# A gated recurrent stage rebuilt on pairs of tiles, in a one-core transformer kernel

## The reference

```python
def step(S, inp):                      # one chunk of 64 rows, for every batch and head
    qb, kb, vb, bb = inp               # bb: running sum of log-sigmoid gates in the chunk
    qg = qb * exp(bb) * scale
    kd = kb * exp(-bb)
    A = where(mask, einsum('bhtd,bhsd->bhts', qg, kd), 0)
    o = einsum('bhts,bhsv->bhtv', A, vb) + einsum('bhtd,bhdv->bhtv', qg, S)
    b_last = bb[:, :, -1:, :]
    kg = kb * exp(b_last - bb)
    S = S * exp(b_last) + einsum('bhtd,bhtv->bhdv', kg, vb)
    return S, o
...
o = o * rsqrt(mean(o * o) + EPS) * rms_w      # per head of 64 columns
o = (o * silu(x @ Wg)) @ Wo
x = x + layernorm(o);  stream = layernorm(x)  # input of the attention layers
```

## Time and profile before

| | |
|---|---|
| median of 3 runs | 548.07 us (546.76 to 548.08) |
| profiled execution | 544.76 us, its span 542.8 us |
| PE busy | 481.8 us (89%), 4512 matmul instructions |
| DVE busy | 407.8 us (75%), 957 |
| ACT busy | 354.8 us (65%), 953 |
| POOL busy | 217.1 us (40%), 188 |
| chain that ended last | PE 50%, DVE 20%, ACT 13%, issue 10%, others 7% |

### The profile page before, as it was taken

The page is one execution under the profiler, slowest core; times in us unless marked ns, Lnnn a source line. Parts: engine busy times, 40 slices in busy tenths (PEclk is TensorE's granted clock), DMA queues, the critical chain, the costliest instruction groups (busy, mean ns, idle before and its releaser), DMA issues.

```text
span 542.8 us, 13374 instructions
## 1 busy us (share of the span) xinstructions
PE 481.8 (89%) x4512; PEld 318.4 (59%) x4512; DVE 407.8 (75%) x957; ACT 354.8 (65%) x953; POOL 217.1 (40%) x188
## 2 busy tenths in 40 slices
PE   3988999997489999999997699799999999987893
PEld 1555655665246767676766356576767676763463
DVE  4799999998377989898985244778888888862456
ACT  3677898886246777777776143476878787752424
POOL 6032111112266666666666001456565656540002
PEclk9999999999589999999999989989999999999798
DMA  6900000000000000000000000000000000000002
GB/s 144 319 0 2 2 2 2 2 2 2 0 1 7 6 12 6 12 6 12 8 11 7 11 0 2 1 1 12 6 11 7 12 7 11 6 13 10 1 0 79
DMA packets 19338, 10.26 MB, mean 19 GB/s; under 512 B 11532, under 2 KB 18504, under 8 KB 19272
## 3 DMA queue, kind: packets, MB, share of 16 engines
q1 hardware_dynamic: 18952, 9.40, 6.2%
q0 software_dynamic: 320, 0.01, 0.2%
HBM read 6.25 MB, written 1.05 MB: 13 GB/s over the span
## 4 chain that ended last, share of the span: by engine, by line
PE 50%; DVE 20%; ACT 13%; issue 10%; DMA 2%; POOL 2%; SPq 2%; DVEq 0%; ACTq 0%; POOLq 0%
PE p_turn L476 11%; PE p_sc L476 9%; PE p_qk L476 8%; PE p_vo L476 8%; DVE ss L1428 4%; DVE neg_max L1445 4%; ACT sq L1036 4%; PE p_mix L476 4%; PE p_turn L704 3%; PE p_sc L744 2%; ACT qk_t L1055 2%; DVE hid L1230 2%; DVE probs L1452 2%; ACT probs_t L1068 2%; POOL qr L426 2%
## 5 line engine op out<-in xcount | busy, mean ns | idle before, releaser
L417 POOL TENSOR_TENSOR qr<-rot 128x1024 f32<-128x1024 f32 x32 | 76.5, 2389 | 104.8 <-DVE rot L1420 104.8
L426 POOL TENSOR_TENSOR qr<-qr,inv 128x1024 f32<-128x1024 f32 x32 | 60.9, 1902 | 41.2 <-issue 38.5
L476 PE MATMUL p_qk<-wqkv_sb,h_t 128*128 128x512 f32 x128 | 63.6, 622 | 5.6 <-ACT sq L1036 4.9
L1428 DVE TENSOR_REDUCE ss<-sq 128x16 f32<-128x1024 f32 x32 | 39.0, 1219 | 34.3 <-ACT sq L1036 34.3
L384 POOL TENSOR_TENSOR og<-og,silu 128x256 f32<-128x256 f32 x16 | 11.6, 726 | 98.9 <-DVE og L1285 98.9
L1061 ACT ACTIVATE probs<-probs 128x512 f32<-128x512 f32 x64 | 40.4, 631 | 13.8 <-DVE probs L1452 13.0
L1075 ACT ACTIVATE o_t<-p_vo 128x512 f32<-128x512 f32 x32 | 19.1, 598 | 42.7 <-PE p_vo L769 42.7
L1452 DVE TENSOR_TENSOR probs<-p_sc,neg_max 128x512 f32<-128x512 f32 x64 | 44.3, 692 | 2.2
L1445 DVE TENSOR_REDUCE neg_max<-p_sc 128x4 f32<-128x512 f32 x64 | 43.7, 683 | 1.8 <-PE p_sc L476 1.8
L704 PEld LDWEIGHTS p_turn<-consts,qr 128*128 128x128 f32 x256 | 29.5, 141 | 24.1 <-POOL qr L426 13.9
L1420 DVE TENSOR_TENSOR rot<-p_qk,cos_t 128x1024 f32<-128x1024 f32 x32 | 38.6, 1207 | 3.4 <-PE p_qk L476 3.4
(11 more groups left out here) (166 smaller groups left out, 1174.8 us busy)
## 6 DMA issues: line engine op xcount, KB each, us to landing
wqkv_sb<-in_L_ffn_wqkv SPq DMA_DIRECT2D x1, 1536.0 KB, 9.7
hcat<-middle SPq DMA_DIRECT2D x32, 32.0 KB
out_x<-pong SPq DMA_DIRECT2D x8, 128.0 KB, 1.9
hcat<-middle SPq DMA_DIRECT2D x32, 31.8 KB
x_in<-in_L_attn_x SPq DMA_DIRECT2D x2, 448.0 KB, 5.2
w_sb<-in_L_ffn_w SPq DMA_DIRECT2D x1, 682.0 KB
cos_base<-rotary_cos SPq DMA_DIRECT2D x1, 512.0 KB, 5.5
sin_base<-rotary_sin SPq DMA_DIRECT2D x1, 512.0 KB, 6.3
```

Source lines behind the costliest of these rows:

```text
L417: pool.tensor_tensor(o, a, b[:, :, ::-1, :], ALU.add).then_inc(s["add_ready"], 1)
L426: pool.tensor_tensor(a, a, inv[:, :].unsqueeze(2).to_broadcast([P, 2 * AH, DH]), ALU.mult).then_inc(s["qr_ready"], 1)
L476: return pe.matmul(o, w, m, start=start, stop=stop, skip_group_check=skip)
L1428: dve.tensor_reduce(ss[:, :], sq[:, :].rearrange("p (h e) -> p h e", e=DH), AX.X, ALU.add).then_inc(s["ss_ready"], 1)
```

## The change

Only the recurrent stage and its seam to attention are changed.

- The unit is now a pair of tiles, one of each batch (256 rows), so there are 8 steps in place of 16, and element-wise instructions are twice as wide.
- Scores, key-value, intra and state products are made for each batch, head and chunk apart: 16 products each per pair, with 32 or 64 contraction rows, on their own part of the array. The padding and the four 32-row instructions of `decay_q` are gone. Within `intra_scores` and `state_outputs` the second half of the heads waits for the first (`at_done`, `half_done`).
- The two low-rank gate matrices are multiplied once at the start (`combine_gate_weights`), and rms_w is folded into Wo.
- The state is kept so that the key product with `kd` serves it (u = S + kd^T v, then S = u * decay, the second on POOL); `kg` and its decay are gone. silu is an exp, ln, exp chain (x clamped at -87 by `gate_input` on DVE).
- `normalise_x`, `normalise_f`, `decay_log`, the state decays and the product of gate and value move from DVE to POOL. The two rotary tables move on POOL from steps 2 and 3 to behind the last `gate_o`, ahead of the last `add_y` and `normalise_f`.
- Attention's first transposes and its first q and k product stand on PE ahead of the last pair's `transpose_o` and `project_out`; on DVE the first rotation stands ahead of the last `normalise_y`.

```diff
+            def intra_scores(t, par):
...
+                for hh in range(2):
+                    wait(pe, s["at_done"], 2 * t + hh)
+                    for b in range(B):
+                        for hp in range(2):
+                            h = 2 * hh + hp
+                            r = slice(h * GDK, (h + 1) * GDK)
+                            for c in range(2):
+                                at = par * PW + b * P + c * CH
+                                ins = mm(bank[4 + hp][c * CH:(c + 1) * CH, head_at(b, h):head_at(b, h) + CH],
+                                         kd[r, at:at + CH], qg[r, at:at + CH])
+                    ins.then_inc(s["at_done"], 1)
...
+            def intra_outputs(t, par):
...
+                for b in range(B):
+                    for h in range(GH):
+                        for c in range(2):
+                            r = slice(c * CH, (c + 1) * CH)
+                            at, v_at = head_at(b, h), par * VW + b * GV + h * GDV
+                            a_at = par * VW + h % 2 * HC + at
+                            ins = mm(bank[6 + h % 2][r, at:at + GDV], a_t[r, a_at:a_at + CH], v_sb[r, v_at:v_at + GDV],
+                                     start=(b == 0 and h < 2), stop=False, skip=True)
...
+                paired(project_gate, k, 1)
...
+                paired(project_out, k, -1)
+                paired(state_outputs, k, 0)
+                paired(project_vg, k, 1)
+                paired(transpose_x, k, 2)
+
+            combine_gate_weights()
+            iterate(pe, gla_step, end=NP)
...
                 def enter():
+                    if l == 0:
+                        pe.wait_ge(s["zero_pool"], 1)
+                        pe.wait_ge(d["d_qkv"], 32)
+                        pe.wait_ge(s["yn_ready"], NP - 1)
                     transpose_in(0, 0)
...
                     enter_on()
+                    gla_transpose_o(NP - 1, (NP - 1) % 2)
+                    gla_project_out(NP - 1, (NP - 1) % 2)
...
+                paired(ln_of_y, k, -1)
+                paired(rstd_of_y, k, -1)
+                paired(gate_exp, k, 0)
+                paired(gate_ln, k, 0)
+                paired(gate_sigmoid, k, 0)
+                paired(square_o, k, 0)
+                paired(copy_v, k, 1)
+                paired(ln_of_f, k, -1)
+                paired(rstd_of_f, k, -1)
+                paired(ln_of_o, k, 0)
+                paired(rstd_of_o, k, 0)
+                paired(copy_xn_t, k, 2)
...
+                paired(stats_x, k, 2)
+                paired(aggregate_x, k, 2)
+                paired(decay_min, k, 1)
+                paired(mask_scores, k, 0)
+                paired(state_0, k, 0)
+                paired(decay_cumulate, k, 1)
+                paired(state_1, k, 0)
+                paired(stats_y, k, -1)
+                paired(aggregate_y, k, -1)
+                paired(decay_k, k, 1)
+                paired(decay_q, k, 1)
+                paired(normalise_y, k, -1)
+                paired(sum_o, k, 0)
+                paired(gate_input, k, 1)
+                paired(stats_f, k, -1)
+                paired(aggregate_f, k, -1)
+                paired(scale_o, k, 0)
...
+                    last = NP - 1
+                    for stage, n in ((stats_y, last), (aggregate_y, last), (rotate, 0), (normalise_y, last),
+                                     (sum_squares, 0), (bound_squares, 0), (stats_f, last), (aggregate_f, last)):
```

More of the change, by code:

```diff
@@ L56, in sems @@
             return {k: ctx.enter_context(nc.semaphore(k)) for k in names.split()}
[L58 to L68, removed]
+        psum = ctx.enter_context(nc.psum_tensor("psum", [P, 8 * 512], F32))
+        p_mix, p_qk, p_vo, p_turn, p_sc = (psum[:, i * 512:j * 512] for i, j in ((0, 1), (1, 3), (3, 4), (4, 6), (6, 8)))
+        bank = [psum[:, i * 512:(i + 1) * 512] for i in range(8)]
+        consts = sb("consts", 6 * P)
+        ident, keep = consts[:, 0:P], consts[:, 2 * P:4 * P]
+        causal_bits = consts[:, P:P + CH].bitcast(U32)
         ident_bf = sb("ident_bf", P, BF16)
@@ L120, in build_program @@
[L120 to L135, removed]
@@ new lines, in gate_o, with add_y @@
+            def gate_o(t, par):
+                wait(pool, s["og1_ready"], t + 1)
+                wait(pool, s["gate_ready"], t + 1)
+                wait(pool, s["ogt_done"], t - 1)
+                c = slice(par * VW, (par + 1) * VW)
+                pool.tensor_tensor(og2[:, c], og1[:, :], gate[:, c], ALU.mult).then_inc(s["og2_ready"], 1)
+            def add_y(t, par):
+                wait(pool, s["yn_ready"], t + 1)
+                pool.tensor_tensor(pair_of(x_attn, t), pair_of(x_in, t), yn[:, par * PW:(par + 1) * PW], ALU.add
+                                   ).then_inc(s["x1_ready"], 1)
@@ L405, in _, with first_tables @@
+            def first_tables():
+                first_cos_table()
+                sin_table(0)
+            iterate(pool, gla_step, end=NP + 1, before={NP: first_tables})
             for l in range(DEPTH):
@@ L570, in transpose_o @@
[L570 to L585 removed]
+            b_xg, b_qk, b_vg = bank[0][:, 0:PW], bank[1], bank[2:4]
@@ new lines, in rstd_of_x, with copy_xn_t @@
+            def rstd_of_x(t, par):
+                wait(act, s["x_ln"], t + 1)
+                wait(act, s["xn_ready"], t - 1)
+                c = slice(par * B, (par + 1) * B)
+                act.activation(rstd_x[:, c], ln_x[:, c], ACT.Exp, scale=-0.5).then_inc(s["x_rstd"], 1)
+            def copy_xn_t(t, par):
+                wait(act, s["xt_done"], t + 1)
+                for read in ("gk_done", "vg_done", "proj_done"):
+                    wait(act, s[read], t - 1)
+                act.activation(xn_t[:, par * PW:(par + 1) * PW], b_xg, ACT.Copy).then_inc(s["xnt_ready"], 1)
@@ L1191, in decay_min, with stats @@
-            def decay_min(n, par):
-                if isinstance(n, int) and n == 0:
+            dve.memset(state[:, 0:B * GDV], 0.0).then_inc(s["zero_state"], 1)
+            dve.memset(a_t, 0.0).then_inc(s["zero_scores"], 1)
+            b_xg, b_qk, b_vg = bank[0][:, 0:PW], bank[1], psum[:, 1024:2048]
+            def stats(buf, st, t, par):
+                for b in range(B):
+                    at = par * B + b
+                    ins = dve.bn_stats(st[:, 6 * at:6 * at + 6], buf[:, b * D:(b + 1) * D])
+                return ins
```

900 lines of the change are left out of this document (440 added, 460 removed).

## The result

The changed kernel took 553.46 us (median of four runs, 551.20 to 555.12) against 547.41 us for the kernel before on the same chip: ratio 1.0133, 95% interval 1.0101 to 1.0165, so slower. The forecast was 552 us. The profiled execution took 555.12 us with a span of 553.3, 10.4 us more than before's, where 3.6 were forecast; the direction was right, and the size in the profile was not.

A forecast was written before the change was run, and what follows sets the result against it. Recurrent stage bound by PE and DVE, both 95% busy, the seam by a chain through all engines. Profiled 544.76, start and steps -1.2, seam +4.8: 548.4; the median lies 3.3 above, so 552 us, range 538 to 565.

The forecast's parts named there:

- What is late next: Pair's step: next gate product waits for ACT's `copy_xn_t`, 7.0 us after the output product; PE stands still 3.7 us.
- The clock: Recurrent steps: the 3.7 us gap loses PE's granted clock each step, adding 1.7 us, so 15.5 us a pair.
- the shorter of two stretches: Behind a 3.77 us gap in the trace: 3.4 us of work at half speed, adding 1.7 us a step.
- the longer case: Behind the other 3.77 us gap: 6.3 us of slow work after work resumed, adding 3.1 us a step.
- PE's work: Pair's step on PE: 6.8 us from gate product to the end of the output product, through at 10.1.
- The start: Start of the recurrent stage: first full step begins at 18.5 us, runs cold and takes 12.1, to 30.6.
- The last pair: Last step: its mask stands behind `scale_o`; 23.9 us with slow stretches, last state product at 132.0 against 133.2.
- The seam: Recurrent stage to attention: late ACT copy and POOL add behind `normalise_f` give 25.1 us against 20.3, 4.8 more.
- Clock holds: Rival, recurrent steps: gaps under 2 us or small products keep the clock; 11.9 us less, 540 us; chance 0.25.
- Clock down throughout: Rival, recurrent steps: clock never recovers, step 17.7 us, 15 us more in total, 567 us; chance 0.12.
- Bank conflict: Rival, `intra_outputs`: row groups writing one bank take turns, 7 us more on any case, 559 us; chance 0.06.
- Entry hides the seam: Rival, attention's entry: its second tile catches up, so the seam is not longer; 4 us less, 548; chance 0.12.

The follow-up runs named there:

- the kernel with the fill, 12 products: Changed kernel plus 12 unread identity products on PE behind the transposes of x in five steps: 541.48 us, ratio 0.991 to the kernel before.
- the kernel with the early copy: Changed kernel with `copy_xn_t` moved right behind `copy_v` in ACT's list: 539.94 us, ratio 0.988 to the kernel before.
- the filled ones: Changed kernel plus unread work on PE behind the transposes of x: 12 identity products 541.48 us, 24 identity transposes 539.16 us.
- the first fill: First place where unread identity products or transposes were added on PE to the changed kernel, behind the transposes of x; those kernels took 539.16 to 549.75 us.
- both seam kernels: Changed kernel with POOL's last `normalise_f` behind the first `scale_qk`, 549.59 us; and with tables, rotation, squares and last pair's norm entries all reordered, 546.08 us.
- 24 products: Changed kernel plus 24 unread identity products on PE behind the transposes of x in five steps: 543.27 us, ratio 0.994 to the kernel before.
- 12 and 24 transposes: Changed kernel plus 12 or 24 identity transposes on PE in place of the filling products: 549.75 us (ratio 1.0077) and 539.16 us (ratio 0.988).
- the full reordering: Changed kernel with tables back in steps 2 and 3, first rotation and squares earlier, last pair's `add_y`, f statistics and `normalise_f` later: 546.08 us, ratio 0.9999.

## Why the prediction was right, and where its sizes were off

**What is late next: right.** Every settled gap of PE was ended by ACT's `copy_xn_t`, 4.0 us of it against 3.7 forecast, and from the end of the output product to the next gate product it was 7.07 us in the step shown (88.75 to 95.82) and up to 7.6 in the others, against 7.0. The step at full clock, seen in the kernel with the fill, is 13.96 us against 13.8: 6.50 and 7.47 us where 6.8 and 7.0 were added up. One term of that sum was not what it seemed: the sigmoid's 1.9 us counted in full, and taking it out gave 0.8, because beside it ran PE's own state and v and gate products, and then `copy_v`. The sum was right since the two paths nearly tie.

**The clock: right in kind, too small.** This is the term that was mis-sized. The prediction took 1.7 us a step, from the shorter of two stretches, and named 3.1 for the longer. The kernel lost 2.6 us a step (16.52, the mean of four steps, less 13.96), and the slow stretches were those of the longer case or more, 6.3 to 6.9 us in three steps and 8.8 in one. The four settled steps missed by 1.0 us each, 0.9 of it the clock, and the first of the five (15.41 us) did not miss; that is the 4.0 us of the table. It turned the sign of the stage: forecast to end 1.2 us earlier than before, it ended 3.8 us later. So the forecast of a slower kernel rested on the seam alone, where the measured one comes from both. The gap at which the clock goes was also read too high: "none below 1.5 did" did not carry over, as a gap of 1.45 us lost it in the kernel with the early copy, while gaps of 1.35 and 1.42 us kept it in seven of the eight whole steps of the filled ones. Nor does length alone decide: seven kernels have the same instructions up to the first fill, with a gap of 1.22 us ahead of the second full step's gate product. Behind it the clock fell in four of the profiled executions (the changed kernel, 12 products, and both seam kernels) and stayed at 1.00 in three (24 products, 12 and 24 transposes). What decides was not settled.

**PE's work: right.** To the end of the output product it took 6.50 us at full clock against 6.8 (59.57 to 66.07 in the kernel with 12 products). The 32-row forms, for which no row stood, went at 1.01 us per 32 instructions with 32 contraction rows and 0.46 with 32 columns, against 1.09 and 0.8 taken. PE's timeline in that kernel:

```profile
59.57 0.70 PE L532 MATMUL psum<-middle,wgk_sb 128*128 128x256 f32 x2 [1.35 <-ACT middle L967]
60.20 1.01 PE L532 MATMUL psum<-middle 32*64 32x64 f32 x32
...
63.06 0.46 PE L532 MATMUL psum<-hid,probs 64*32 64x64 f32 x32
63.83 1.15 PE L532 MATMUL psum<-hid 64*64 64x64 f32 x32 [0.31 <-ACT pong L1044]
64.91 1.16 PE L532 MATMUL psum<-wout_sb,pong 128*128 128x128 f32 x8
```

**The start: right.** 19.16 against 18.5, and the cold first step exactly 12.1. That agreement is luck: the clock stood at 1.00 when the step began and fell only at 26 us, so that the v and gate product took 3.45 us and not 1.98. In eleven of the twelve experiments that step took 10.0 to 10.5 us, the clock held through it, and in five of them nothing ahead of its end was changed. The chance of a warm first step was not in the forecast.

**The last pair: right in size.** It took 24.2 us against 23.9, but PE's gap of 4.96 us there was ended by POOL's `gate_o`, and not by the mask. Both paths are nearly as long: the copy behind the mask was done at 130.48, `gate_o` at 130.75.

**The seam: right in its mechanism.** 26.5 us against 25.1: rotation 14.4 us behind the last state product (14.0), POOL's first add 7.8 behind the rotation (6.8). Moving `normalise_f` alone gave 3.5 to 3.9 us back, 2.3 of it in the seam, and moving all of it 8.9 us of the seam.

**The rivals.** Clock holds: its condition was not met. The filled kernels, in which it mostly or always held, reached 541.5 and 539.2 us where 540 was forecast, but its price was low: 12.0 and 14.3 us less than the changed kernel, for 11.9. Clock down throughout: fell, the clock came back in each step. Bank conflict: fell; the 32 instructions of `intra_outputs` took 1.15 us at full clock, 36 ns each against 34 for the nearest row, and 1.97 at half clock. Their two row halves write one bank, but other partitions of it. Entry hides the seam: false for this kernel (389.8 us behind it, before 389.3), though part of what the full reordering saved was given back there, 2.0 us.

Why 552 came so near with 6.7 us missed in the profile (548.4 against 555.12): the prediction added 3.3 us for the distance of before's median from its profiled run, and the changed kernel's median lies 1.7 us below its profiled one. Two errors of opposite sign met, and that the total fell so close is luck. Of the four runs two took 555 us at a mean clock of 0.912 and 0.921, and two 551 and 552 at 0.933 and 0.930, so the clock's share changes from run to run by itself.

## What to carry to other kernels

When a change empties two full engines, look for what they wait for now: read the chain through the in-order lists from the last consumer back to the first, and put what the next product needs ahead of what nobody waits for. An idle stretch of TensorE costs a second time where the clock falls behind it, in the work that is on the path; dummy work in the gap shows within one run how much of the time is clock. A table or a norm that fits in an engine's idle time is free only behind the entry for which others wait, not ahead of it.

## What the runs showed of the hardware

- Transposes of 128x128 hold the clock as products do, if they fill the same time: 24 in 2.78 us, the clock at 1.00 in the four whole steps behind them.
- The same work can keep the clock or lose it: behind the same gap of 1.22 us it fell in four profiled executions and held in three.
- A float32 product of 128 columns takes two instructions of 118 ns, a transpose one of 116 ns; the one fills twice the time of the other.
- `bound_squares` on DVE, 16 columns in SBUF, took 1.43 us beside POOL's add of 1024 columns and ended with it, against 0.17 us alone. That the two share something is inferred from this one place.
- Row tiles that write the same bank in different partitions did not slow each other (36 ns an instruction).
